# Decay sums of a delta-rule kernel as three bfloat16 products in place of one float32 product

## The reference

```python
g = -jnp.exp(A_log) * jax.nn.softplus(x @ Wa.T + dt_bias)      # log decay of each token and head, [B, L, H]
g_full = zeros([B, L, 2, H]); g_full[:, :, 0] = g               # the first of the two steps of a token decays
def step(state, inp):                                           # T = 2 L = 256 steps, B = 8, H = 8
    q_t, k_t, v_t, g_t, b_t = inp
    state = state * jnp.exp(g_t)[..., None, None]
    corr = jnp.einsum('bhk,bhkv->bhv', k_t, state)
    v_new = (v_t - corr) * b_t[..., None]
    state = state + jnp.einsum('bhk,bhv->bhkv', k_t, v_new)
    return state, jnp.einsum('bhk,bhkv->bhv', q_t, state)
```

## Time and profile before

| what | value |
|---|---|
| three runs | 603.48, 611.27, 611.97 us |
| median | 611.27 us |
| the profiled execution | 603.35 us |
| its span | 601.6 us |
| TensorE busy in the span | 557.3 us (93%) |
| VectorE busy | 455.2 us (76%) |
| ScalarE busy | 357.8 us (59%) |
| POOL busy | 38.3 us (6%) |

### The profile page before, as it was taken

One profiled execution on the slowest core, in us unless ns is written; L12 is line 12 of the kernel. 1 busy time (PEld: TensorE's weight loads), 2 busy tenths in 40 slices (PEclk: granted clock), 3 DMA queues, 4 the chain that ended last, 5 costly groups with the idle time before them and its releaser, 6 DMA issues.

```text
span 601.6 us, 15363 instructions
## 1 busy us (share of the span) xinstructions
PE 557.3 (93%) x6484; PEld 377.7 (63%) x6484; DVE 455.2 (76%) x1066; ACT 357.8 (59%) x559; POOL 38.3 (6%) x66
## 2 busy tenths in 40 slices
PE   8799889999999999999999999999998799668997
PEld 5445347576657665766576667666666688556646
DVE  5778997797778877887788778878796535589663
ACT  2684766594659466946694668465864144187351
POOL 5340000100010001000100010010000000100000
PEclk9989999999999999999999999999998699968999
DMA  6001021102110200020002101210013400000002
GB/s 166 2 20 31 21 63 25 23 10 40 41 22 11 69 10 22 13 68 11 21 14 66 12 20 17 65 13 19 2 36 70 127 3 12 1 0 1 2 0 70
DMA packets 49700, 18.63 MB, mean 31 GB/s; under 512 B 39100, under 2 KB 48352, under 8 KB 49632
## 3 DMA queue, kind: packets, MB, share of 16 engines
q1 hardware_dynamic: 49632, 17.66, 12.2%
HBM read 14.49 MB, written 3.15 MB: 29 GB/s over the span
## 4 chain that ended last, share of the span: by engine, by line
PE 75%; DVE 11%; ACT 7%; issue 2%; SPq 1%; DMA 1%; POOL 0%; ACTq 0%; DVEq 0%
PE bank L1290 18%; PE bank L1340 7%; DVE acc L888 6%; PE bank L1470 4%; PE bank L1466 4%; PE bank L1238 4%; PE bank L1561 4%; PE bank L1343 3%; PE bank L1359 3%; PE bank L1482 3%; PE bank L1425 3%; PE bank L1476 3%; PE bank L1478 2%; PE bank L1480 2%; PE bank L1337 2%
## 5 line engine op out<-in xcount | busy, mean ns | idle before, releaser
L888 DVE SCALAR_TENSOR_TENSOR acc<-bank,cw,acc 128x508 f32<-128x508 f32 (+2 forms) x240 | 176.5, 739 | 36.3 <-ACT acc L592 32.1
L1290 PE MATMUL bank<-xnT,wq 128*128 128x512 f32 x320 | 154.9, 610 | 12.6 <-DVE acc L888 11.6
L1290 PEld LDWEIGHTS bank<-xnT,wq 128*128 128x128 f32 x320 | 56.3, 191 | 71.3 <-issue 43.4
L592 ACT ACTIVATE acc<-bank,cw 128x512 f32<-128x512 f32 x80 | 55.3, 691 | 52.7 <-PE bank L1290 50.4
L1340 PE MATMUL bank<-kq 128*128 128x384 f32 x128 | 49.9, 497 | 0.0
L639 ACT ACTIVATE T<-bank 32x512 f32<-32x512 f32 (+1 forms) x32 | 18.9, 590 | 41.9 <-PE bank L1359 29.0
L607 ACT ACTIVATE vT<-acc 128x512 f32<-128x512 f32 x32 | 21.0, 671 | 37.5 <-DVE acc L888 37.4
L921 DVE SCALAR_TENSOR_TENSOR AM<-bank,rb,DT 128x384 f32<-128x384 f32 x64 | 37.6, 608 | 1.8 <-PE bank L1340 1.5
L989 DVE SCALAR_TENSOR_TENSOR xres<-bank,f,xres 128x256 f32<-128x256 f32 x64 | 26.9, 478 | 8.6 <-PE bank L1470 8.3
L607 ACT ACTIVATE kq<-acc 128x512 f32<-128x512 f32 x48 | 31.6, 660 | 2.2 <-DVE acc L888 1.9
L1470 PE MATMUL bank<-wo,oTh 128*128 128x256 f32 x128 | 31.9, 383 | 0.0
(11 more groups left out here) (247 smaller groups left out, 1085.1 us busy)
## 6 DMA issues: line engine op xcount, KB each, us to landing
wq<-in_w_qkv SPq DMA_DIRECT2D x8, 640.0 KB, 4.1
blocks<-AM SPq DMA_DIRECT2D x128, 8.0 KB, 1.5
xres<-in_x SPq DMA_DIRECT2D x2, 512.0 KB, 4.5
Yl<-in_y_init SPq DMA_DIRECT2D x8, 128.0 KB, 2.4
Bl<-blocks SPq DMA_DIRECT2D x8, 128.0 KB, 2.0
wg<-in_w_gate SPq DMA_DIRECT2D x8, 128.0 KB, 2.1
solved<-Yl SPq DMA_DIRECT2D x8, 128.0 KB, 1.7
Yc<-solved SPq DMA_DIRECT2D x64, 16.0 KB, 1.9
```

What stands on the lines that cost most here:

```text
L592: a(acc[:, u % RING, :, :], bank[6 + u % 2][:, :].rearrange("p (b l) -> p b l", b=4), ACT.Copy, scale=cw[:, t, 3:4]).then_inc(s_tap.next(f ...
L888: stt(w, ps[:, :, 0:L - s], cw[:, t, 3 - s:4 - s], w, ALU.mult, ALU.add).then_inc(s_cv.next(f"u{u}_{s}"), 1)
L1290: ins = mm(bank[6 + u % 2][:, :], wq[:, cc, t, :], xnT[:, cc, 512 * half:512 * half + 512], start=cc == 0, stop=cc == KC - 1)
```

## The change

The log decays gl are split once, on POOL, into three bfloat16 parts gl3 whose sum is the float32 value. decay_rows spreads all three: Gb becomes bfloat16 with 3 x 8 x 128 = 3072 columns, by one operation a head as before. The zeros and ones of seg are cast once to bfloat16 (pastb, on VectorE), and each decay sum is three bfloat16 products that accumulate in the tile, then the masking product as before. In the first head the decay sums move behind unit 9 on TensorE, and so do their exponentials behind tap 9 on ScalarE. To make room in SBUF, twice, seg and bsig, which are used only ahead of head 0's solve, now lie in W1.

```diff
-FIRST_SCALAR_ORDER = ("... q1 +8 dt0 +9 dt1 dt2 cs nr -6 -7 -8 -9").split()
+FIRST_SCALAR_ORDER = ("... q1 +8 +9 dt0 dt1 dt2 cs nr -6 -7 -8 -9").split()
-FIRST_TENSOR_ORDER = ("0 1 2 3 4 5 6 7 8 dt0 dt1 9 dt2 ca cs nrm e1_0 ...
+FIRST_TENSOR_ORDER = ("0 1 2 3 4 5 6 7 8 9 dt0 dt1 dt2 ca cs nrm e1_0 ...
...
+        pastb = sb("pastb", [P, 2, P], BF16)
-        Gb = sb("Gb", [P, B, L])
+        Gb = sb("Gb", [P, 3, B, L], BF16)
+        gl3 = sb("gl3", [P, 3, B, H], BF16)
...
+        twice = W1[:, 0:NH, :]
+        seg = W1[:, 4:6, :]
+        bsig = W1[:, 6:8, :].rearrange("p k (c n h) -> p (k c) n h", n=2, h=H)
...
             pool.wait_ge(s_preG.sem, s_preG.at("gl"))
+            pk(g.tensor_copy(gl3[:, 0, :, :], gl[:, :, :]))
+            pk(gt(r2, gl[:, :, :], gl3[:, 0, :, :], ALU.subtract))
+            pk(g.tensor_copy(gl3[:, 1, :, :], r2))
+            pk(gt(r2, r2, gl3[:, 1, :, :], ALU.subtract))
+            pk(g.tensor_copy(gl3[:, 2, :, :], r2))
...
-                g.tensor_tensor(Gb[:, :, :], rep(lower.rearrange("p (o l) -> p o l", o=1), 1, B), rep(gl[:, :, hs], 2, L), ALU.mult).then_inc(s_gb.next("gb"), 1)
+                g.tensor_tensor(Gb[:, :, :, :].rearrange("p k b l -> p (k b) l"), rep(lower.rearrange("p (o l) -> p o l", o=1), 1, 3 * B),
+                                rep(gl3[:, :, :, hs].rearrange("p k b o -> p (k b) o"), 2, L), ALU.mult).then_inc(s_gb.next("gb"), 1)
...
                 v.tensor_copy(segb[:, :, :], cst[:, 4:6, :])
+                v.tensor_copy(pastb[:, :, :], seg)
...
                 elif name == "dt2":
-                    mm(o, seg[:, 1, :], Gb[:, :, 64:L], start=True, stop=False)
+                    for part in range(3):
+                        mm(o, pastb[:, 1, :], Gb[:, part, :, 64:L], start=part == 0, stop=False)
...
                 elif name[:2] == "dt":
-                    mm(o, seg[:, 0, :], Gb[:, 4 * i:4 * i + 4, :], start=True, stop=False)
+                    for part in range(3):
+                        mm(o, pastb[:, 0, :], Gb[:, part, 4 * i:4 * i + 4, :], start=part == 0, stop=False)
```

More of the change, by code:

```diff
@@ L89 @@
 E_STEPS = " ".join(f"e1_{2 * i} e1_{2 * i + 1} e2_{i}" for i in range(4))
-FIRST_SCALAR_ORDER = ("+0 +1 -0 +2 +3 -1 +4 +5 -2 q0 -3 +6 -4 +7 -5 q1 +8 dt0 +9 dt1 dt2 cs nr -6 -7 -8 -9").split()
+FIRST_SCALAR_ORDER = ("+0 +1 -0 +2 +3 -1 +4 +5 -2 q0 -3 +6 -4 +7 -5 q1 +8 +9 dt0 dt1 dt2 cs nr -6 -7 -8 -9").split()
 FIRST_VECTOR_ORDER = ("u u u u u u u u u u u u u u u u u u u u u u u u u u u u u u rb e1_0 e1_1 e2_0 e1_2 rq e1_3 e2_1 e1_4 "
                 "e1_5 e2_2 e1_6 e1_7 e2_3 vt0 vt1 vt2 vt3").split()
-FIRST_TENSOR_ORDER = ("0 1 2 3 4 5 6 7 8 dt0 dt1 9 dt2 ca cs nrm e1_0 e1_1 e2_0 e1_2 e1_3 e2_1 e1_4 e1_5 e2_2 e1_6 e1_7 "
+FIRST_TENSOR_ORDER = ("0 1 2 3 4 5 6 7 8 9 dt0 dt1 dt2 ca cs nrm e1_0 e1_1 e2_0 e1_2 e1_3 e2_1 e1_4 e1_5 e2_2 e1_6 e1_7 "
                 "e2_3 vt0 vt1 vt2 vt3").split()
@@ L179, in build @@
         vT = sb("vT", [P, B, 2 * L])
-        seg = sb("seg", [P, 2, P])
+        pastb = sb("pastb", [P, 2, P], BF16)
         segb = sb("segb", [P, 2, P], BF16)
@@ L185, in build @@
         beta = sb("beta", [P, CH, H])
-        bsig = sb("bsig", [P, CH, 2, H])
         gl = sb("gl", [P, B, H])
@@ L191, in build @@
         tokb = sb("tokb", [P, B, 16])
-        twice = sb("twice", [P, NH, P])
         al = sb("al", [P, H])
@@ L371, in _ @@
                 sp.dma_start(dst, src).then_inc(s_first.next(name), 16)
-            loads = [(seg[:, :, :], consts.rearrange("k p n -> p k n")[:, 6:8, :]), (cm[:, :], masks),
+            loads = [(seg, consts.rearrange("k p n -> p k n")[:, 6:8, :]), (cm[:, :], masks),
                      (al[:, :], a_log), (dtb[:, :], dt_bias),
```

## The result

| | before | changed |
|---|---|---|
| median of 11 runs each | 611.27 us (603.48 to 613.54) | 618.34 us (613.29 to 620.97) |
| profiled execution, its span | 603.35, 601.6 us | 620.9, 619.1 us |

The changed kernel is slower: 7.1 us by the medians (1.0116), and 1.0215 by the ratio, with a 95% interval of 1.017 to 1.0261. The medians take all executions, the ratio only those that were in the same state of the chip, and of the kernel before it goes by a base near 605.3 us (618.34 / 1.0215), low in its range. So that it is slower is clear, and whether by more or less than 2% is not.

What follows compares the result with a forecast made beforehand. TensorE, without slack in the steady heads, was taken as the bound. Five steady heads, head 7 and head 0 gave 6 D - 26.3 = +6.7 us at D = 5.5, on the 611.3 us median: 618.0 us, range 607.7 to 621.6.

Steps and rivals of the forecast that it cites:

- Gb on POOL: POOL's decay rows of each head: 3072 columns take 5.5 us instead of 1.913 us.
- idle of dt0, heads 2 to 6: TensorE ahead of dt0 in steady heads: waits 1.89 us for Gb, 5.5 us against 3.61 us of cover.
- saving of the three sums: TensorE, each head's three decay sums: bfloat16 products save 0.8 us, between 0.64 and 1.04.
- head 0, tap 8 to colsum: Head 0, ScalarE: tap 9 ahead of dt0 and the table load makes colsum 1.0 us later (0.7 to 1.5).
- The second rival: POOL's Gb: mixed operand costs over 2.1 ns a column, kernel over 2% slower, 627 us at 7 us; chance 0.17.
- the first: POOL's Gb: half the bytes keep it under 3.6 us, ready in time; -3.8 us, 607.5; chance 0.12.
- The fourth: TensorE's decay sums: each bfloat16 product reloads weights in the open, 1.8 us more a head, +17 us; chance 0.03.
- The third rival: TensorE behind the stalls: longer idle lowers its clock, some 2 us a head, +17 us, 628; chance 0.04.
- D: Duration of the changed Gb operation on POOL, taken as 5.5 us; counts six times in the sum.
- Head 1: Head 1: no stall, as Gb is written 22 us before use, and no gain, as the chain runs through ScalarE; zero.
- lower corner: Whole kernel: Gb 5.38 us, saving 1.04, head 0 at 0.7, given as +4.3 us.
- within 2%: Whole kernel's measured time against before: change within 2%, chance 0.78; slower by over 2% 0.20, faster 0.02.

Runs made afterwards that it cites:

- experiment 4: Changed kernel with head 0's old order on TensorE and ScalarE (dt0 and dt1 ahead of unit 9): 619.17 us, ratio 1.0184.
- experiment 3: Kernel before, float32 sums, with two more POOL operations of 896 columns ahead of each Gb: 619.71 us, ratio 1.0183.
- experiment 2: Changed kernel, POOL writing head h + 2's decay rows ahead of its wait for ly, behind head h's last substitution step: 608.65 us, ratio 0.9987.
- 6: Kernel before, with POOL writing decay rows as soon as dt2 of the head ahead is filled, beside the substitution: 611.21 us, ratio 1.0035.
- 8: Kernel before, float32 sums, with POOL's list as in experiment 2: 610.56 us, ratio 0.9911.
- 5: Changed kernel with the edits of experiment 2 and experiment 4 together: 607.60 us, ratio 0.9961.
- 9: Kernel of 5, with head 1's rows also waiting until VectorE has used head 0's first product, behind rb: 610.50 us, ratio 0.9995.
- 10: As 9, but with the changed kernel's first order (unit 9 and tap 9 ahead of dt0): 611.99 us, ratio 1.0048.
- 11: As 9, but head 1's rows wait until VectorE has scaled rq of head 0: 605.11 us, ratio 0.9971.

## Why the prediction was right

The forecast was 618.0 us, the median is 618.34. Its parts, each against what was measured:

| step | forecast | measured |
|---|---|---|
| Gb on POOL | 5.5 us (5.38 to 5.74) | 5.375 us, eight times |
| idle of dt0, heads 2 to 6 | 1.89 us | 1.66 us, five times; by dt0's start behind Gb's 5.43 - 3.61 = 1.82 us |
| idle of dt0, head 7 | 1.03 us | 0.90 us |
| saving of the three sums | 0.8 us (0.64 to 1.04) | 0.81 us by the chain where the rows are in time, 0.7 to 0.9 by distances |
| net by steady head | +1.1 us | +0.9 to +1.1 us |
| head 0, tap 8 to colsum | +1.0 us | 8.47 - 7.26 = +1.2 us, and rb +0.25 us |

**Price of Gb.** The slope through the 256 and 1024 column rows held within 10 ns (1.913 + 2048 x 0.001695 = 5.384 against 5.375 us); a bfloat16 operand costs POOL nothing here. The second rival (dearer columns) falls with that, and so does the first (half the bytes). The fourth (weights reloaded in the open) falls with the 0.75 us of three products on the chain.

**The clock behind a stall.** The third rival is not refuted; it came in part. The clock fell right behind dt0's wait in one of the five steady heads of the changed kernel (head 2) and in two of the five of experiment 4, and in none of experiment 3. Each time the distance was 1.3 to 1.6 us longer, and not the 2 us in every head that I priced. I had argued from one pair of idles, 3.30 us with the clock low behind it and 1.91 us with the clock full. The runs don't bear such a border out: the same idle of 1.91 us in head 1, at full clock before, was followed in the changed kernel by a granted clock of 0.58 (80 to 84 us), and in experiments 2, 6 and 8 the clock fell in a steady head behind other idles of 1.1 to 1.2 us, with no stall of dt0. So the stalls were followed by the lower clock in 3 of 15 heads. The kernel before and those of experiments 2, 5, 8, 9, 10 and 11, which have no stall of dt0 and no hold there, show it in 2 of 35 heads. Whether the stalls make it more frequent these few can't tell.

**The stall and the saving, taken apart.** The distances of steady heads form a square. It holds the first four distances of each kernel, without the four whose mean granted clock was 0.97 (60.66 in experiment 2, 61.60 in 8, 61.67 in the changed kernel, 62.00 in 4); all others had 1.00:

| | rows in time | rows late |
|---|---|---|
| float32 sums | 59.2 to 59.6 (before, 8) | 61.0 to 61.6 (3) |
| bfloat16 sums | 58.3 to 59.1 (2, 5, 9, 10, 11) | 60.2 to 60.7 (changed, 4) |

By the middles of the squares (59.4, 61.3, 58.7, 60.4), the sums save 0.7 and 0.9 us down the columns, and the late rows cost 1.9 and 1.7 us along the rows. By the trace the saving, where the rows are in time, is 0.21 us for dt0, 0.31 for dt1 (1.06 to 0.75) and 0.29 for dt2 (1.05 to 0.76), 0.81 us: half of the merges' extra, as I had taken it. That the stall adds in full, with no slack behind it, was argued from a wait of 1.7 us in 260; experiment 3 shows it. The recorded idle is 0.2 us under the forecast, of which 0.125 is D. The idle is not the whole price, though: I had subtracted dt0's saving in full, and behind the wait its products take 0.82 and not 0.65 us. In the changed kernel a steady head thus pays 1.66 + 0.82 - 0.86 = 1.62 us at dt0 and gets back 0.31 and 0.29, which leaves +1.0 us, as the distances have it.

**Head 0.** The size held: colsum is 1.2 us later behind tap 8 than before. That tap 9 ahead of the table load is the whole price didn't hold. With the old order and the longer rows dt0 waits for them, and from tap 8 to colsum it took 7.7 to 8.2 us (experiments 4, 5, 9, 11) against 7.26 before, so 0.4 to 1.0 us come with either order. The other half of the balance I had as a side remark: what the old order would gain is taken by rb being held (experiment 4), so the order itself cost the kernel nothing that shows.

**Head 1.** I counted zero. The changed kernel's first Yc is 2.7 us later, 1.45 of it from head 0 and 0.6 already there at tap 8 (39.76 against 39.16), ahead of the changed order; tap 8 came between 38.8 and 42.4 us in the profiles. The rest, some 0.6 us, comes with the clock of 0.58 in 80 to 84 us, where the kernel before had 1.00. No stall and no gain of head 1 shows. Experiment 3 had its first Yc 3.0 us later than before as well, but it is no measure of chance alone: its gl ended 1.8 us later, and its rb ran into POOL's added work and float32 rows and took 1.91 us, up to 50.92, 0.04 us behind the rows.

**The forecast of the pair.** I said 610.1 us for an execution like the profiled one, and the profiled one took 620.9. Of the 17.5 us between the pair some 7 are the terms above, 8.0 are the tail at the lower clock, 1.4 the clock behind head 2's stall, and some 1.2 lie in head 0 ahead of tap 8 and in head 1. The choice of the median as base, against the profiled execution at the low edge of the runs, was what made the number come out; the sum itself can't tell this. With executions that spread over 8 to 10 us, that it came within 0.4 us of the median is luck; what the runs bear out is the sum of +6.7 us against terms of some 7. (The lower corner of that sum is 4.2 and not 4.3 us.)

**What I got wrong in kind.** I gave "within 2%" 0.78. The medians agree, the ratio of 1.0215 is at the bound. And the obvious mend, which the prediction implied (write the rows earlier), costs 5.4%: I had named the contention of POOL and VectorE and priced it at half a microsecond in one place (rb, where it took 0.25), since in the steady heads the long Gb happened to lie beside convolution steps that read PSUM. It was that cover, not its length, that kept the change near 1%.

## What to carry to other kernels

When work moves to an idle engine, ask two things of its new length: what stands ahead of it in that engine's list and who waits for its end (here 3.6 us of cover against 5.4), and which instructions of the neighbour engine run beside it. Here POOL work was free beside VectorE's work from PSUM, and beside small SBUF-only steps in a serial chain it cost nearly its full length (5.1 of 5.4 us). To place it, wait on the end of that chain rather than on the first moment at which the data may be overwritten. And where the bottleneck engine has no slack, a saving and a new stall add up head by head, so here 0.7 to 0.9 us of saving a head was bought with 1.7 to 1.9 us of waiting.

## What the runs showed of the hardware

- In the rows shown, a VectorE instruction with two SBUF operands, or a tensor_scalar with one, that started while POOL's rows were being written ended 0.03 to 0.08 us behind them: it took 5.34 instead of 0.21 us, 1.89 and 0.82 instead of 0.21, 1.61 instead of 0.19, and 3.54 instead of 0.17. A reciprocal on SBUF and the convolution steps and products with an operand in PSUM kept their durations. POOL's own instruction never got longer: 5.37 to 5.38 us in every place.
- POOL's tensor_tensor costs the same a column with a bfloat16 operand and result as with float32: 1.913 us for 1024 columns, 5.375 for 3072.
- Three bfloat16 products of 512 columns behind 64-row merges have 0.75 us on the chain, a float32 one 1.06; behind another 128-row product they have 0.65 against 0.86, and behind a wait of 1.66 us 0.82. Behind the merges they pay 0.1 us more, the float32 one 0.2; that this is the load of the weights is argued, not shown.
- The same idle of TensorE was followed by either level of the clock: 1.91 us in head 1 by 1.00 in the kernel before and by 0.58 in the changed one, 1.66 us by 0.50 in head 2 and by 1.00 in heads 3 to 6 of the same execution.
- The same last stretch of the kernel took 57.2 to 65.3 us in thirteen profiles, with granted clocks between 0.50 and 1.00 in its windows.
